# First scores by halves of the key/query ring, and row maxima turned by VectorE, in a fused transformer layer on one core

## The chip, the core and the metric

The kernel runs on one core of a Trainium2 chip. The metric is the device time of one execution in microseconds (us). TensorE (PE) does matmuls, VectorE (DVE) elementwise work and reductions, ScalarE (ACT) activations and copies, GpSimd (POOL) elementwise work, and SyncE (SP) only starts DMAs. ACT and POOL can start DMAs too. Every engine runs its own instructions in order, and semaphores tie the engines together. PSUM is the memory that TensorE writes: eight banks of 512 floats in each of 128 partitions.

## The reference, cut to what matters

```
x = x + attention(layernorm(x))     # 4 x 512 x 256, 16 heads of 16, biases, softmax over 512 keys
x = x + ffn(layernorm(x))           # silu(x W1') * (x W3'), Walsh-Hadamard transform over 1024, W2'
x = x + memory(layernorm(x))        # gate, scan with decay 0.95, query, output
x = x + ffn(layernorm(x))
scores  = einsum("bhqd,bhkd->bhqk", Q, K) / sqrt(16)
softmax = exp(scores - max over k) / sum over k
```

All of it is float32. The kernel splits each float32 operand into a high part (float32r) and a low part (the rest) and adds three products of parts, so that TensorE can run in its faster float32r form.

## The kernel before, in words

**Attention.** Batch `b` has 8 head pairs and 4 tiles of 128 tokens, so 32 steps (`STEPS`), and the loop variable `K` counts 128 steps over the four batches, with `s = K % 32`. A head of 16 channels stands as 48 rows in `ring`: three products of high and low parts of queries (`QI`) and keys (`KI`). Two heads share the 128 partitions: rows 0 to 47 (`blk` 0) and 64 to 111 (`blk` 1). `HALF` is 64. Rows `MROW` = 48 and 49 of each half hold minus the row maxima of the scores (high and low part) on the query side and ones on the key side, so that a second matmul over 50 rows gives score minus maximum.

**Two passes.** `score_qk(U, h)` computes queries by keys for step `U` and half `h`, into one of three banks (3 to 5), and DVE takes its negated maximum (`row_max`, tile `mxr`). `score_kq(K, h)` computes keys by queries with the maximum folded in, ACT takes the exponential (L735), and `weigh_values` multiplies by the values (`Vp`). The first pass runs 13 steps ahead (`LEAD`), so 26 scores are done before step 0. Eight steps make a group `S`, whose 16 columns of maxima must have become rows of `ring` before step `8 S`.

**How maxima become rows.** POOL splits the group's maxima into `ms` (L1071 and L1073, `split_max`), at steps with `s % 8 == 3`. TensorE transposes `ms` (L440, L472) into bank 7 (`MB`), which projections and others share, at `s % 8 == MAX_AT`. ACT copies it to `mT` (`max_evacuate`). SP starts two DMAs of `mT` into the rows (`max_rows`). Step `8 (S+1)` waits for `mrow_in`.

**Start.** DMAs bring in x, weights and constants. TensorE runs seven matmuls of ones (`keep_busy`) and then transposes the normalised first batch `XNs` (L396) as its four tiles come from DVE (`first_xns`). The projections follow: query and key tiles `n` = 0 to 3, of which 0 and 1 are the first heads' queries and keys, and then the values. ACT and DVE make the high and low parts `qh` and `ql` (for `n` = 2 and 3 in `AOh` and `AOl`), and DMAs spread them over `ring`: SP for `n` = 0, ACT for `n` = 1 (L704), six DMAs each. The first score waits for all twelve. `fly` is a butterfly on POOL for W2's Walsh-Hadamard transform (L1119, L1120), finished by four matmuls with `had` (`HAD_AT`) and two ACT copies each.

**Beside attention.** Projections of the next batch and of the output run inside the loop in `shared_bank`. POOL adds `ql`, `xTl`, `W2l` (L1051), the normalisation of the next batch (L1054; in batch 0 at `s` = 24 to 27, `NORM_AT`), `divide` (L1090) and the values' bias (L1080). Each is placed by step, and each engine takes them in the order of its loop body. TensorE transposes the next batch's `XNs` at `s` = 30 (`LN_AT[0]`, L292) and waits there for `xns_ready`.

After step 127 come the two FFNs and the memory layer; no line of theirs is touched.

Of the kernel before, what the change touches and what calls it, by code (L numbers as in the profile page):

```python
# [11 lines left out]
P = 128  # L12
# [5 lines left out]
GROUPS = 4  # L18
# [15 lines left out]
MAX_AT = 5  # L34
# [13 lines left out]
HAD_AT = (4, 5, 6, 8)  # L48
# [6 lines left out]
def build(nc, x, wq, wk, wv, wo, bqk_d, bv, bo, mv_, mg, mq, bgq_d, mo, w1, w2, w3, ident_d, had_d, out):  # L55
    ctx = ExitStack()
    with ctx:
# [36 lines left out]
        ms = sb("ms", [P, 2, 2, 2 * TT])  # L94
        mT = sb("mT", [32, P])
# [8 lines left out]
        spare = sb("spare", [P, 1])  # L104

# [19 lines left out]
        def quarter(slot, i):  # L125
# [5 lines left out]
        first_xns, wq_in, wk_in = (sem(n) for n in ("first_xns", "wq_in", "wk_in"))  # L131
# [12 lines left out]
        s1_ready, max_done, mh_done, ml_done, mps_ready, mt_ready, mrow_in = (  # L144
            sem(n) for n in ("s1_ready", "max_done", "mh_done", "ml_done", "mps_ready", "mt_ready", "mrow_in"))
# [11 lines left out]
        out_done = sem("out_done")  # L157
# [31 lines left out]
        def _(sp):  # L189
# [49 lines left out]
            max_rows(0)  # L239
            for b in range(BATCH):  # L240
# [38 lines left out]
        def _(pe):  # L279
# [55 lines left out]
            def score_qk(U, h):  # L335

                b, p, t = U // STEPS, U % STEPS // TT, U % TT
                i, blk = 2 * U + h, 1 - h
# [11 lines left out]
            def wait_qk(U, h):  # L350
                if U % 16 == 0 and h == 0:
                    b, mt = U // STEPS, U % STEPS // 16
                    pe.wait_ge(ring_in[2 * mt], QDMAS * (b + 1))
                    pe.wait_ge(ring_in[2 * mt + 1], QDMAS * (b + 1))
# [3 lines left out]
            def wait_kq(K, h):  # L358
                if K % 8 == 0 and h == 0:
                    pe.wait_ge(mrow_in, 2 * DMA * (K // 8 + 1))  # L360
                if K == 0 and h == 0:
                    pe.wait_ge(ones_in, 4 * DMA)
                j = 2 * K + h
# [7 lines left out]
            def weigh_values(a):  # L371
                S, kt = a // 4, a % 4
                g = S % GROUPS
                pe.wait_ge(exp_done, 4 * a + 4)
                if kt == 0:
# [15 lines left out]
            keep_busy(7, MB, SEQ)  # L391
# [9 lines left out]
            keep_busy(1, MB, SEQ)  # L401
# [16 lines left out]
            for U in range(LEAD):  # L418
                for h in range(2):
                    wait_qk(U, h)  # L420
                    score_qk(U, h)
                if U == 4:

                    pe.wait_ge(fly_done, 3)
                    pe.wait_ge(v_copied, 2)
                if U in HAD_AT:
                    j = HAD_AT.index(U)
                    mm(PS[:, HAD_BANK[j], :], had[:, :], PR[:, 4 + j, :], True, True).then_inc(had_ready, 1)
                elif U < 8:
                    keep_busy(1, MB, FILL)  # L430
                elif U == LEAD - 2:
                    pe.wait_ge(xns_ready, 1)
                    pe.wait_ge(mt_ready, 1)
                    ln_transpose(0, MB)
                else:
                    pe.wait_ge(w2h_done, 3)
                    keep_busy(1, PS[:, 2, :], FILL)
                if U == 8:
                    pe.wait_ge(ml_done, 1)
                    nc.tensor.transpose(MB[0:32, 0:P], ms[:, :, :, :].rearrange("p a b k -> p (a b k)"), ident[:, :])\  # L440
                        .then_inc(mps_ready, 1)
            pe.wait_ge(w2h_done, FT // 2)

            def shared_bank(K, b, s):

                more, turned = b < BATCH - 1, K + LEAD
                if s == LN_AT[0] and more:

                    pe.wait_ge(xns_ready, b + 2)
                    pe.wait_ge(mt_ready, turned // 8)  # L450
# [4 lines left out]
                if s % 8 == MAX_AT:  # L455
                    S = turned // 8 - 1
                    if S < LAST_GROUP:
                        pe.wait_ge(ml_done, S + 1)
                        pe.wait_ge(mt_ready, S)
                        if s // 8 == 0 and more:  # L460
                            pe.wait_ge(qk_f, 4 * b + 1)
                        elif s // 8 == 0:
                            pe.wait_ge(x_f, 2 * (b + 1))
                        elif s // 8 == 1 and more:
                            pe.wait_ge(qk_f, 4 * b + 3)
                        elif s // 8 == 2 and more:
                            pe.wait_ge(v_copied, 2 * (b + 1) + 1)
                        elif s // 8 == 2:
                            pe.wait_ge(x_done, 2 * b - 1)
                        elif more:  # L470
                            pe.wait_ge(v_copied, 2 * (b + 2))
                        nc.tensor.transpose(MB[0:32, 0:P], ms[:, :, :, :].rearrange("p a b k -> p (a b k)"),  # L472
                                            ident[:, :]).then_inc(mps_ready, 1)
                for n in range(4):
                    if s in QK_AT[n] and more:
                        if s == QK_AT[n][0]:
                            if n == 0:
                                pe.wait_ge(x_f, 2 * (b + 1))
                            elif n == 2:
                                pe.wait_ge(qk_f, 4 * b + 2)  # L480
                            else:
                                pe.wait_ge(mt_ready, turned // 8)
                        i = 3 * QK_AT[n].index(s)
                        project_qk(b + 1, n, range(i, i + 3))
                if s == OUT_AT[0][0] and b:
# [3 lines left out]
                    else:  # L489
                        pe.wait_ge(mt_ready, turned // 8)  # L490
                    for part in range(2):
                        out_projection(0, part)
                if s in OUT_AT[1] and b:
                    if s == OUT_AT[1][0]:
                        pe.wait_ge(mt_ready, turned // 8)
# [8 lines left out]
                if s in V_AT[1] and more:  # L504
                    if s == V_AT[1][0] and b:
                        pe.wait_ge(x_done, 2 * b)
                    elif s == V_AT[1][0]:
                        pe.wait_ge(mt_ready, turned // 8)
# [133 lines left out]
        def _(act):  # L642
# [17 lines left out]
            def qk_split(b, n):  # L660
                act.wait_ge(qk_f, 4 * (b - 1) + n + 1)
                act.wait_ge(ring_in[(n + 2) % 4], QDMAS * (b + (n > 1)))
# [7 lines left out]

            def max_evacuate(S):
                act.wait_ge(mps_ready, S + 1)
                if S:
                    act.wait_ge(mrow_in, 2 * DMA * S)
                hi(mT[:, :], MB[0:32, 0:P]).then_inc(mt_ready, 1)
# [20 lines left out]
            for n in range(4):  # L696
# [3 lines left out]
                if n == 1:  # L700
                    for part, ready in ((0, qk_hi), (1, qk_lo)):
                        act.wait_ge(ready, 2)
                        for args in ring_rows(0, 1, part):
                            act.dma_start(*args).then_inc(ring_in[1], DMA)  # L704
            for half in range(2):
                v_evacuate(0, half, PS[:, V_BANK[half], :])
            for n in range(2):
                act.wait_ge(ring_in[n], QDMAS)
# [519 lines left out]
```

## Time and profile before

| | us |
|---|---|
| median of 3 runs | 586.35 (586.34 to 586.47) |
| the profiled execution's own time | 586.26 |
| its span, first to last instruction | 584.4 |
| TensorE busy | 565.8 (97% of the span) |
| VectorE, ScalarE, GpSimd busy | 376.8, 298.5, 176.6 |
| granted TensorE clock over the span | 0.999 |

Busy time of an engine is the union of its instructions. TensorE's records overlap, so its busy share does not tell how much it streams; where one piece of its work ends and the next begins is read from starts. The time outside the span is 586.26 - 584.4 = 1.86 us.

### The profile page before, as it was taken

The page shows a single profiled execution, that of the slowest core. Times are in us where ns is not written, and L with a number is a line of the kernel's source. Part 1 is how long each engine was busy: PE and PEld are TensorE (multiplying, and loading weights), DVE is VectorE, ACT ScalarE, POOL GpSimd, SP SyncE. Part 2 cuts the span into 40 slices and gives each one's busy share as a digit, 9 for nine tenths or more (in the row PEclk, how much of TensorE's full clock was granted, in tenths as well). Part 3 has the DMA queues.
Part 4 walks back from the last instruction along what each step waited for, and adds up shares of the span by engine and source line. Part 5 has one row for each costly group of instructions (what it writes and reads, how often), then busy time and mean ns, then how long its engine had stood idle before and what let it go on. Part 6 is the DMA issues. An engine that isn't in the chain of part 4 may idle for free.

```text
span 584.4 us, 8867 instructions
## 1 busy us (share of the span) xinstructions
PE 565.8 (97%) x3288; PEld 390.1 (67%) x3288; DVE 376.8 (64%) x718; ACT 298.5 (51%) x546; POOL 176.6 (30%) x193
## 2 busy tenths in 40 slices
PE   9899999999999988999999999999999999999997
PEld 4534334344334433368888888898777888888886
DVE  5498898898888899644363444558887436344433
ACT  3238878876886787752334242244445233424221
POOL 3956446354455242820101010014333010101000
PEclk9999999999999999999999999999999999999999
DMA  7654740240033030010000000000000010010101
GB/s 231 135 112 163 199 122 18 76 127 20 2 111 109 3 146 3 3 72 2 1 0 1 1 0 1 2 2 0 1 0 2 1 36 1 1 36 2 38 0 37
DMA packets 17891, 26.54 MB, mean 45 GB/s; under 512 B 2552, under 2 KB 10744, under 8 KB 17464
## 3 DMA queue, kind: packets, MB, share of 16 engines
q1 hardware_dynamic: 15992, 24.13, 13.6%
q10 hardware_dynamic: 1856, 1.84, 1.4%
q8 instruction: 27, 0.44, 0.3%
q14 instruction: 16, 0.13, 0.1%
HBM read 10.88 MB, written 5.24 MB: 28 GB/s over the span
## 4 chain that ended last, share of the span: by engine, by line
PE 85%; DVE 5%; ACT 4%; issue 2%; DMA 1%; POOL 1%; SPq 1%; DVEq 0%; ACTq 0%
PE PS L281 82%; PE PS L292 2%; DVE mxr L861 2%; ACT PR L735 1%; DMA ring<-ql 1%; DVE PR L1020 1%; ACT xf L644 1%; ACT qf L658 1%; DVE XNs L842 1%; ACT PR L788 1%; POOL xTl L1051 1%; ACT xTh L644 1%; PE PS L472 1%; DVE AOl L853 1%; SPq L214 1%
## 5 line engine op out<-in xcount | busy, mean ns | idle before, releaser
L281 PE MATMUL PS<-xTh,ring 128*128 128x512 f32 x608 | 188.5, 392 | 0.0
L861 DVE TENSOR_REDUCE mxr<-PS 128x1 f32<-128x512 f32 x256 | 163.0, 682 | 29.0 <-PE PS L281 28.7
L735 ACT ACTIVATE PR<-PS 128x512 f32<-128x512 f32 x256 | 137.8, 603 | 39.7 <-PE PS L281 39.7
L281 PEld LDWEIGHTS PS<-xTh,ring 128*128 128x128 f32 x608 | 113.2, 188 | 22.9 <-issue 0.8
L281 PE MATMUL PS<-xTl,ring 128*128 128x512 f32 x304 | 110.3, 391 | 0.4 <-POOL xTl L1051 0.4
L281 PE MATMUL PS<-ring 50*128 50x512 f32 (+1 forms) x512 | 98.2, 450 | 5.4 <-DVE mxr L861 4.9
L975 DVE TENSOR_TENSOR PR<-PR,PS 128x512 f32<-128x512 f32 x64 | 43.8, 684 | 91.6 <-PE PS L281 73.7
L281 PEld LDWEIGHTS PS<-ring 50*128 50x128 f32 (+1 forms) x512 | 41.2, 184 | 84.2 <-ACT PR L735 57.2
L644 ACT ACTIVATE AOh<-PR 128x512 fp32r<-128x512 f32 x72 | 45.5, 632 | 101.1 <-DVE PR L975 89.2
L1051 POOL TENSOR_TENSOR xTl<-xf,xTh 128x512 fp32r<-128x512 f32 x30 | 43.2, 1456 | 140.9 <-ACT xTh L644 140.9
L853 DVE TENSOR_TENSOR AOl<-PR,AOh 128x512 fp32r<-128x512 f32 x72 | 51.1, 710 | 50.3 <-ACT AOh L644 50.3
L773 ACT ACTIVATE PR<-PS 128x512 f32<-128x512 f32 x64 | 38.0, 594 | 82.7 <-PE PS L281 82.6
L281 PE MATMUL PS<-W2h,AOh 128*128 128x256 f32 x256 | 72.4, 283 | 0.0
L281 PE MATMUL PS<-W2l,AOh 128*128 128x256 f32 x256 | 72.4, 283 | 0.0
L281 PE MATMUL PS<-W2h,AOl 128*128 128x256 f32 x256 | 72.2, 282 | 0.0
L281 PE MATMUL PS<-PR,Vp 128*32 128x512 f32 x512 | 68.2, 604 | 1.8 <-ACT PR L735 1.6
L281 PEld LDWEIGHTS PS<-xTl,ring 128*128 128x128 f32 x304 | 57.0, 188 | 11.0 <-POOL xTl L1051 0.8
L281 PEld LDWEIGHTS PS<-W2h,AOl 128*128 128x128 f32 x256 | 48.9, 191 | 1.9
L281 PEld LDWEIGHTS PS<-W2l,AOh 128*128 128x128 f32 x256 | 48.9, 191 | 1.9
L281 PEld LDWEIGHTS PS<-W2h,AOh 128*128 128x128 f32 x256 | 48.9, 191 | 0.0
L1044 POOL TENSOR_TENSOR veps<-mom,eps 128x4 f32<-128x4 f32 x16 | 3.2, 200 | 128.4 <-DVE mom L832 128.3
L1090 POOL TENSOR_TENSOR OTn<-OT,rec 128x256 f32<-128x256 f32 x16 | 9.9, 620 | 64.2 <-DVE rec L908 64.2
(98 smaller groups left out, 621.5 us busy)
## 6 DMA issues: line engine op xcount, KB each, us to landing
ring<-qh SPq DMA_DIRECT2D x52, 128.0 KB, 3.1
ring<-ql SPq DMA_DIRECT2D x26, 128.0 KB, 3.1
ring<-weight_scratch SPq DMA_DIRECT2D x3, 1024.0 KB, 4.9
weight_scratch<-in_w SPq DMA_DIRECT2D x2, 1024.0 KB, 6.8
out<-X SPq DMA_DIRECT2D x8, 256.0 KB, 2.2
X<-in_x SPq DMA_DIRECT2D x3, 512.0 KB, 5.2
PR<-in_w SPq DMA_DIRECT2D x1, 1024.0 KB, 7.6
ring<-AOh SPq DMA_DIRECT2D x8, 128.0 KB, 4.0
```

The source lines that it names most:

```text
L214: sp.dma_start(*args).then_inc(ring_in[n], DMA)
L281: return nc.tensor.matmul(dst, lhsT, rhs, start=start, stop=stop, skip_group_check=True)
L292: last = nc.tensor.transpose(bank[:, t * P:(t + 1) * P], XNs[:, t, dt * P:(dt + 1) * P], ident[:, :])
L472: nc.tensor.transpose(MB[0:32, 0:P], ms[:, :, :, :].rearrange("p a b k -> p (a b k)"), ident[:, :]).then_inc(mps_ready, 1)
L644: return nc.scalar.activation(dst, src, ACT.Copy, scale=scale)
L735: nc.scalar.activation(PR[:, j % 8, :], PS[:, kq_bank(j), :], ACT.Exp, scale=HD ** -0.5)\
L773: nc.scalar.activation(PR[:, f % 2, :], PS[:, f % 2, :], ACT.Silu).then_inc(sg_done, 1)
L853: return nc.vector.tensor_tensor(dst, src, h.bitcast(F32), ALU.subtract)
L861: nc.vector.tensor_reduce(mxr[:, S % 2, blk, TT * p + t:TT * p + t + 1], PS[:, QK0 + i % 3, :], AX.X, ALU.max, negate=True).then_inc(max_d ...
L975: nc.vector.tensor_tensor(PR[:, 2 + f % 2, :], PR[:, f % 2, :], PS[:, 2 + f % 2, :], ALU.mult)\
L1051: return nc.gpsimd.tensor_tensor(dst, src, h.bitcast(F32), ALU.subtract)
L1090: nc.gpsimd.tensor_tensor(OTn[:, :, c:c + HD], OT[:, :, 0:HD], rec[:, :].unsqueeze(2).broadcast_to([P, SEQ // 32, HD]), ALU.mult)\
```

## The change

**Scores.** `score_qk` takes every fourth query (`t:SEQ:TT`) as its stationary operand instead of 128 neighbours. The first 16 scores come in the order: all eight steps of half `h` = 0 (`blk` 1), and then all eight of `h` = 1 (`first_score`). **Ring rows.** SP starts all twelve first DMAs, those of `blk` 1 ahead of those of `blk` 0, with a semaphore for each half (`first_rows`); ACT starts none. The eight DMAs of `wo` move from ACT to SP, behind the first group's maxima. **Maxima.** `ms` becomes 128 x 4 x 32 and is zeroed once; DVE transposes it in blocks of 32 x 32 into `mT` (`turn_max`); TensorE's transposes and ACT's copies of maxima go. The rows are moved by eight DMAs of one row and four partitions each: four from SP and four from POOL (`max_rows` on POOL, directly behind `split_max`). **Start.** `keep_busy` is 4 instead of 7 matmuls at first, and 1 instead of 5 ahead of the scores; the matmuls with `had` move to steps 8, 9, 10 and 12; the normalisation of batch 1 moves from POOL to ACT (two passes of four activations); the parts of `WO` are made in steps 3 and 5.

```diff
-MAX_AT = 5
+MAX_AT = 4
-HAD_AT = (4, 5, 6, 8)
+HAD_AT = (8, 9, 10, 12)
-        ms = sb("ms", [P, 2, 2, 2 * TT])
-        mT = sb("mT", [32, P])
+        ms = sb("ms", [P, TT, 32])
+        mT = sb("mT", [P, P])
+        def first_score(i):
+
+            return (i % 8, i // 8) if i < 16 else (i // 2, i % 2)
+
+        def max_row_copies(S, blk):
+
+            b, g = S // GROUPS, S % GROUPS
+            return [(ring[HALF * blk + MROW + k:HALF * blk + MROW + k + 1, b % 2, QI, 2 * g + p, :].bitcast(F32),
+                     mT[16 * p + 2 * blk + k:P:32, :]) for k in range(2) for p in range(2)]
...
             def max_rows(S):
-
-                b, g = S // GROUPS, S % GROUPS
                 sp.wait_ge(mt_ready, S + 1)
-                for blk in range(2):
-                    r = HALF * blk + MROW
-                    sp.dma_start(ring[r:r + 2, b % 2, QI, 2 * g:2 * g + 2, :].bitcast(F32),
-                                 mT[16 * blk:16 * blk + 16, :]).then_inc(mrow_in, DMA)
+                for to, src in max_row_copies(S, 0):
+                    sp.dma_start(to, src).then_inc(mrow_in, DMA)
...
-            ring_load(0, 0)
-
-            for n in range(2):
-                sp.wait_ge(ring_in[n], QDMAS)
+
+            for blk in (1, 0):
+                for n in range(2):
+                    copies = ring_rows(0, n, 0)[2 * blk:2 * blk + 2]
+                    sp.wait_ge(qk_hi, n + 1)
+                    for args in copies:
+                        sp.dma_start(*args).then_inc(first_rows[blk], DMA)
+                    copies = ring_rows(0, n, 1)[blk:blk + 1]
+                    sp.wait_ge(qk_lo, n + 1)
+                    for args in copies:
+                        sp.dma_start(*args).then_inc(first_rows[blk], DMA)
             ring_load(0, 2)
             ring_load(0, 3)
             max_rows(0)
+
+            for e in range(2):
+                for j in range(GH):
+                    r = 32 * j + HD * e
+                    sp.dma_start(OT[r:r + HD, :, :].rearrange("p a c -> p (a c)").rearrange("p (g n) -> p g n", n=D),
...
-                mm(PS[:, QK0 + i % 3, :], ring[r:r + KROWS, b % 2, QI, p, t * P:(t + 1) * P],
+
+                mm(PS[:, QK0 + i % 3, :], ring[r:r + KROWS, b % 2, QI, p, t:SEQ:TT],
...
-            keep_busy(7, MB, SEQ)
+            keep_busy(4, MB, SEQ)
...
-            keep_busy(1, MB, SEQ)
+            keep_busy(1, MB, FILL)
...
-            keep_busy(2, PS[:, 5, :], SEQ)
-            pe.wait_ge(ring_in[0], QDMAS)
-            keep_busy(3, PS[:, 5, :], SEQ)
+            keep_busy(1, PS[:, 5, :], SEQ)
             pe.wait_ge(qk_hi, 4)
             pe.wait_ge(qk_lo, 4)
...
-                if s % 8 == MAX_AT:
-                    S = turned // 8 - 1
-                    if S < LAST_GROUP:
-                        pe.wait_ge(ml_done, S + 1)
-                        pe.wait_ge(mt_ready, S)
...
-                        nc.tensor.transpose(MB[0:32, 0:P], ms[:, :, :, :].rearrange("p a b k -> p (a b k)"),
-                                            ident[:, :]).then_inc(mps_ready, 1)
...
+            act.wait_ge(nmean_done, 1)
+            act.wait_ge(rstd_done, 2)
+            act.wait_ge(lnT_ready, 2)
+            for t in range(TT):
+                nc.scalar.activation(XNs[:, t, :], X[:, TT + t, :], ACT.Identity, bias=nmean[:, t:t + 1])\
+                    .then_inc(centred, 1)
...
             for j in range(FT // 2):
                 if j == FT // 2 - 1:
-                    max_evacuate(0)
+                    ln_evacuate(1, 0, MB)
+                    ln_hi(1, 0, 0)
...
+            def turn_max(S):
+
+                dve.wait_ge(ml_done, S + 1)
+                if S:
+                    dve.wait_ge(mrow_in, 4 * DMA * S)
+                    dve.wait_ge(mrow_in2, 4 * DMA * S)
+                nc.vector.transpose(mT[:, :].rearrange("p (i t) -> p t i", t=TT), ms[:, :, :]).then_inc(mt_ready, 1)
...
+                if s % 8 == 3 and (K + 5) // 8 < LAST_GROUP:
+                    turn_max((K + 5) // 8)
...
+            def max_rows(S):
+
+                pool.wait_ge(mt_ready, S + 1)
+                for to, src in max_row_copies(S, 1):
+                    pool.dma_start(to, src).then_inc(mrow_in2, DMA)
...
                 if s % 8 == 3 and (K + 5) // 8 < LAST_GROUP:
                     split_max((K + 5) // 8)
+                    max_rows((K + 5) // 8)
```

TensorE's program at the first scores. `AOf` is the tile of ones of `keep_busy`, `ring` the scores. Before:

```order
L281 MATMUL PS<-AOf 128x512 x2
L281 MATMUL PS<-AOf 128x512 [waits ring_in0]
L281 MATMUL PS<-AOf 128x512 x2
L281 MATMUL PS<-ring 128x512 [waits ring_in0,ring_in1,qk_lo,qk_hi]
L281 MATMUL PS<-ring 128x512
L281 MATMUL PS<-AOf 128x384
```

The changed kernel at the same place:

```order
L305 MATMUL PS<-AOf 128x512
L305 MATMUL PS<-ring 128x512 [waits first_rows1,qk_lo,qk_hi]
L305 MATMUL PS<-ring 128x512
L305 MATMUL PS<-AOf 128x384
L305 MATMUL PS<-ring 128x512
L305 MATMUL PS<-ring 128x512 [waits max_done]
```

Four matmuls of ones have gone, and the first score waits for one half's rows instead of two tiles' rows.

POOL's program at the end of batch 0 (`s` = 26 to 28): the third tile of the normalisation, the split of the maxima, the low part of the attention output, the last tile of the normalisation (which signals `xns_ready`) and the values. Before:

```order
L1054 TENSOR_SCALAR XNs<-X,mom,rstd 128x256
L1071 CAST ms<-mxr 128x2x8 [waits mps_ready,max_done]
L1073 TENSOR_TENSOR ms<-mxr,ms 128x2x8 [waits mh_done]
L1051 TENSOR_TENSOR AOl<-AOf,AOh 128x512 [waits aoh_done]
L1054 TENSOR_SCALAR XNs<-X,mom,rstd 128x256
L1080 TENSOR_TENSOR Vp<-vst,bvt 128x4x4x16 [waits av_done,v_copied] x2
```

The changed kernel:

```order
L1061 TENSOR_SCALAR XNs<-X,mom,rstd 128x256
L1082 CAST ms<-mxr 128x2x2x4 [waits mt_ready,max_done]
L1084 TENSOR_TENSOR ms<-mxr,ms 128x2x2x4 [waits mh_done]
L1090 DMA ring<-mT 1x4x128 [waits mt_ready]
L1090 DMA ring<-mT 1x4x128 x3
L1058 TENSOR_TENSOR AOl<-AOf,AOh 128x512 [waits aoh_done]
L1061 TENSOR_SCALAR XNs<-X,mom,rstd 128x256
L1097 TENSOR_TENSOR Vp<-vst,bvt 128x4x4x16 [waits av_done,v_copied] x2
```

Four DMAs, behind a wait for DVE's transpose, now stand ahead of the last tile of the normalisation.

DVE's program at steps 9 to 12 of the changed kernel (before, the same rows without `mT<-ms`):

```order
L909 STREAM_TRANSPOSE OT<-PS 128x512 [waits wol_done,av_done]
L857 TENSOR_REDUCE mxr<-PS 128x1 [waits s1_ready] x2
L913 RECIPROCAL rec<-OT 128x16 [waits ot_done]
L857 TENSOR_REDUCE mxr<-PS 128x1 [waits ml_done,s1_ready]
L857 TENSOR_REDUCE mxr<-PS 128x1 [waits s1_ready]
L866 STREAM_TRANSPOSE mT<-ms 128x4x32 [waits mrow_in2,mrow_in,ml_done]
L857 TENSOR_REDUCE mxr<-PS 128x1 [waits s1_ready] x12
```

The new transpose waits for POOL's split (`ml_done`), and twelve maxima are queued behind it.

## Rows read from the trace of the kernel before

**Rows 1.** By stretch: length, busy PE, PEld, DVE, ACT, POOL; clock, DMA share, GB/s.

```profile
96.74:151.26 54.52, 53.83 (x345) 23.42 (x341) 47.41 (x86) 42.95 (x85) 25.28 (x31) 1.00 0.19 60
251.00:584.40 333.40, 327.35 (x1896) 286.32 (x1896) 172.87 (x350) 120.91 (x200) 48.20 (x46) 1.00 0.03 10
```

**Rows 2.** Chain that ended last, to 45 us: start us, us, what.

```profile
1.44 8.74 PE PS L281 x14
...
18.20 6.24 DMA ring<-ql
```

**Rows 3.** Timeline, 6 to 21 us: start us, us, engine, line.

```profile
6.89 1.38 DVE L842 TENSOR_SCALAR XNs<-X,mom,rstd 128x256 f32<-128x256 f32 x4 [1.48 <-POOL rstd L1047]
8.72 0.63 ACT L644 ACTIVATE WAh<-xf 128x512 fp32r<-128x512 f32 x1 [0.65 <-DMA xf<-in_wv]
11.65 1.09 ACT L644 ACTIVATE xTh<-PS 128x512 fp32r<-128x512 f32 x2 [2.30 <-PE PS L396]
14.94 2.57 SPq L214 DMA_DIRECT2D ring<-qh  x4
```

**Rows 4.** Timeline of PE, 12 to 46 us.

```profile
12.70 0.40 PE L281 MATMUL PS<-xTh,WAh 128*128 128x512 f32 x1
12.94 0.39 PE L281 MATMUL PS<-xTh,WAl 128*128 128x512 f32 x1
...
20.95 1.88 PE L281 MATMUL PS<-AOf 128*128 128x512 f32 x4
24.48 2.84 PE L281 MATMUL PS<-AOf 128*128 128x512 f32 x6 [1.65 <-DMA ring<-ql]
27.25 0.50 PE L281 MATMUL PS<-ring 48*128 48x512 f32 x2
...
28.53 0.51 PE L281 MATMUL PS<-ring 48*128 48x512 f32 x2
...
33.84 0.50 PE L281 MATMUL PS<-ring 48*128 48x512 f32 x2
...
35.33 0.51 PE L281 MATMUL PS<-ring 48*128 48x512 f32 x2
...
44.78 0.74 PE L281 MATMUL PS<-ring 50*128 50x512 f32 x4
```

**Rows 5.** Timeline of PE, steps 5 and 7 (51 to 57 us), and its weight loads.

```profile
51.98 0.74 PE L281 MATMUL PS<-ring 50*128 50x512 f32 x4
...
53.12 1.07 PE L281 MATMUL PS<-PR,Vp 128*32 128x512 f32 x8
...
55.67 0.74 PE L281 MATMUL PS<-ring 50*128 50x512 f32 x4
55.67 0.30 PEld L281 LDWEIGHTS PS<-ring 50*128 50x128 f32 x4 [0.36 <-ACT PR L735]
56.34 1.07 PE L281 MATMUL PS<-PR,Vp 128*32 128x512 f32 x8
```

**Rows 6.** Timeline of DVE and POOL, step 11.

```profile
62.70 1.29 DVE L861 TENSOR_REDUCE mxr<-PS 128x1 f32<-128x512 f32 x2
...
64.91 0.22 POOL L1073 TENSOR_TENSOR ms<-mxr,ms 128x16 fp32r<-128x16 f32 x1
```

**Rows 7.** Timeline of POOL and PE, steps 27 to 30.

```profile
91.28 0.22 POOL L1073 TENSOR_TENSOR ms<-mxr,ms 128x16 fp32r<-128x16 f32 x1
...
92.72 1.22 POOL L1054 TENSOR_SCALAR XNs<-X,mom,rstd 128x256 f32<-128x256 f32 x1
...
94.49 0.66 PE L292 MATMUL PS<-ident,XNs 128*128 128x128 f32 x4
```

**Rows 8.** Tile `mT`, and POOL by form: count, min/median/max ns; busy us, mean ns.

```profile
L222 SPq DMA_DIRECT2D ring<-mT x32: 610/654/686, 40.1 to 239.2; - x32
...
L1047 POOL TENSOR_TENSOR rstd<-veps,mhalf 128x4 f32<-128x4 f32 x16 | 16.2, 1014 | 1.3
```

**Rows 9.** Chain that ended last, step 119.

```profile
239.20 1.92 DMA ring<-mT
```

More of the change, by code:

```diff
@@ L143, in build @@
         ring_in = [sem(f"ring_in{n}") for n in range(4)]
[L144 to L145 removed]
+        first_rows = [sem(f"first_rows{blk}") for blk in range(2)]
+        s1_ready, max_done, mh_done, ml_done, mt_ready, mrow_in = (
+            sem(n) for n in ("s1_ready", "max_done", "mh_done", "ml_done", "mt_ready", "mrow_in"))
         st_ready, exp_done, av_done, ot_done, rec_done, otn_done, aof_ready, aoh_done, aol_done, wo_ready, x_done = (
@@ L442, in _ @@
-            pe.wait_ge(w2h_done, FT // 2)
+            for i in range(2 * LEAD):
+                U, h = first_score(i)
+                if i in (0, 8):
+                    pe.wait_ge(first_rows[1 - h], QDMAS)
+                if i >= 3:
+                    pe.wait_ge(max_done, i - 2)
+                score_qk(U, h, i)
+                if i % 2 and U < 8:
+                    keep_busy(1, MB, FILL)
+                elif i % 2:
+                    if U == 8:
+                        pe.wait_ge(fly_done, 3)
+                        pe.wait_ge(v_copied, 2)
+                    if U in HAD_AT:
+                        j = HAD_AT.index(U)
+                        mm(PS[:, HAD_BANK[j], :], had[:, :], PR[:, 4 + j, :], True, True).then_inc(had_ready, 1)
+                    if U == LEAD - 2:
+                        pe.wait_ge(xns_ready, 1)
+                        ln_transpose(0, MB)
@@ L493, in shared_bank @@
                 if s in OUT_AT[1] and b:
-                    if s == OUT_AT[1][0]:
-                        pe.wait_ge(mt_ready, turned // 8)
+                    if s == OUT_AT[1][0] and more:
+                        pe.wait_ge(v_copied, 2 * (b + 1) + 1)
+                    elif s == OUT_AT[1][0]:
+                        pe.wait_ge(x_done, 2 * b - 1)
                     out_projection(1, OUT_AT[1].index(s))
@@ L699, in _ @@
                     .then_inc(qk_hi, 1)
[L700 to L704, printed above, removed]
             for half in range(2):
                 v_evacuate(0, half, PS[:, V_BANK[half], :])
-            for n in range(2):
-                act.wait_ge(ring_in[n], QDMAS)
-            for e in range(2):
-                for j in range(GH):
-                    r = 32 * j + HD * e
-                    act.dma_start(OT[r:r + HD, :, :].rearrange("p a c -> p (a c)").rearrange("p (g n) -> p g n", n=D),
-                                  wo.rearrange("(g e) (j c) n -> e j c g n", e=2, c=32)[e, j, 0:HD, :, :])\
-                        .then_inc(wo_in, DMA)
+            act.wait_ge(nmean_done, 1)
[4 more added lines that the diff above has]
+                    .then_inc(centred, 1)
+            for t in range(TT):
+                c = slice(TT + t, TT + t + 1)
+                act.wait_ge(centred, t + 1)
+                last = nc.scalar.activation(XNs[:, t, :], XNs[:, t, :], ACT.Copy, scale=rstd[:, c])
+            last.then_inc(xns_ready, 1)
             for j in range(FT // 2):
                 if j == FT // 2 - 1:
-                    max_evacuate(0)
+                    ln_evacuate(1, 0, MB)
+                    ln_hi(1, 0, 0)
                 act.wait_ge(had_ready, j + 1)
@@ L893, in _ @@
                     .then_inc(qk_lo, 1)
-            for U in range(LEAD):
-                for h in range(2):
-                    row_max(U, h)
+            for i in range(2 * LEAD):
+                row_max(*first_score(i), i)
+                if i == 16:
+                    turn_max(0)
             def transpose_out(S):
```

120 lines of the change are left out of this document (45 added, 75 removed).

## The prediction

> **What bounds the kernel now.** I read the windows by stretch first, since a share over the whole span hides stages with different limits. From 251 us on, TensorE is busy 327 of 333 us and every other engine about half of that or less [rows 1]; no line of that stage is touched, so I cost it at nothing. Inside a batch TensorE is again nearly always busy, but VectorE is busy 47.4 of 54.5 us and ScalarE 43.0 [rows 1]: TensorE bounds, with VectorE's maxima close behind. Next the chain that ended last, for the start: TensorE's fills to 10 us, projections, then a DMA of `ring` that lands 6.24 us after its issue [rows 2]. The timeline shows what this costs: the values end at 20.95, fills and an idle gap of 1.65 us follow, the first score starts at 27.25 and step 0 at 44.78 [rows 4]. Last come the steps with `s % 8` of 3 and 5, one with the split, one with TensorE's transpose [rows 5, 6], and the end of batch 0, where POOL's last normalised tile comes just ahead of the matmuls that need it [rows 7].
>
> **The change, part by part: before the first score.** Fourteen records of fills (two for each of seven matmuls) run to 1.44 + 8.74 = 10.18 us, slower before the clock is granted in full [rows 2]. Eight records would end near 7.4. Not all of that comes back: `XNs` is ready at 6.89 + 1.38 = 8.27, and ACT is held by weights from a DMA until 8.72 + 0.63 = 9.35 before it can copy `xTh`, which it started at 11.65 [rows 3]. So `xTh` moves 2.3 us earlier, with a shorter fill 2.4, and all projections with it. SP's issues of rows started at 14.94, four of them in 2.57, so 0.64 each [rows 3]. They now start at 12.5, and the six of `blk` 1 (the other tile's among them) are issued by about 16.3. The values end at 20.95 - 2.4 = 18.55; a fill takes about 0.5 more, and low parts are ready by then. The DMA of rows that took 6.24 us ran with all twelve, at full DMA load. Six ought to land within some 3 us, by 19.3. I take the first score at 19.5, 7.7 us earlier. The other half's six are issued by 20.1, land by about 23.2, and are wanted eight scores later, at 25.5: hidden, with 2 us of cover.
>
> **From the first score to step 0.** Before, a round of two scores and a fill took 28.53 - 27.25 = 1.28 us, one with `had` 35.33 - 33.84 = 1.49 [rows 4]. The two scores of a round stood in different halves of the rows and ran side by side: 0.50 us for both. In the new order the first eight rounds take both from one half, one after the other; consecutive matmuls of 512 columns start 0.24 apart (12.70, 12.94) [rows 4]. So I add 0.23 to 1.28: eight rounds of 1.50, 12.0 us. Then come three rounds with `had` (4.5), one with neither (1.0), one more with `had` (1.5): 19.0 us, against 44.78 - 27.25 = 17.53. Step 0 starts at 19.5 + 19.0 = 38.5, 6.3 us earlier. ACT's last copies of `W2h` now stand later, behind `xTh` of batch 1, and cost the first exponentials an estimated 0.6. **Start: -5.7.** POOL's part (butterfly, then split, then rows) ends some 5 us ahead of step 0, at any price of its DMAs up to 1.3 us.
>
> **Inside the batches: what goes.** A step with TensorE's transpose of maxima takes 53.12 - 51.98 = 1.14 us to its values' matmuls, one without 56.34 - 55.67 = 0.67 [rows 5]: 0.47 back. Two of four per batch are like that; in the other two a projection stands beside it and my reading there is 0.38. That is 1.70 per batch. In batch 0 the last disappears in a stall (below), 1.32; in batch 3 TensorE waits more often for VectorE and I count 0.44. ACT's copies lie in its idle time.
>
> **What comes, on VectorE.** `turn_max` moves 128 x 128 floats, an estimated 0.35 us with its wait. It waits for POOL's split, and behind it are queued the maxima that TensorE's scores wait for (a ring of three banks). At step 11 the previous maxima end at 62.70 + 1.29 = 63.99 and the split at 64.91 + 0.22 = 65.13 [rows 6]: VectorE stands 1.14 us, then turns for 0.35. The banks cover about 1.1 of it; I put 0.4 on TensorE. It happens at step 11 of batches 0 to 2 and step 19 of batch 0: 1.6. At the other steps POOL is ready first.
>
> **What comes, on POOL.** Four DMAs per group. No row shows a DMA from POOL. The nearest are SP's, of the same tiles, at a median 0.654 us of queue time each; a tiny POOL instruction of 128 x 4 takes 1.014 [rows 8]. I take c = 0.8 each, between them; below 0.61 there is no reason to go, upwards there is no firm bound. Their main victim is the end of batch 0. The split ends at 91.28 + 0.22 = 91.50, then come `AOl` (to 92.72) and the last `XNs` (1.22, to 93.94), and TensorE's four transposes at 94.49 [rows 7]. Now the turn (0.35) and 4c stand in between: 91.50 + 0.35 + 4c + 1.22 + 1.22, with semaphores 94.35 + 4c, is 97.55 at c = 0.8. TensorE waits **3.06 us** (2.5 at 0.65, 3.9 at 1). In later batches the normalisation stands at `s` = 19 and is done before.
>
> The rows themselves must land before the next step with `s % 8` = 0. A DMA of `mT` lands 1.92 us from the start of its issue [rows 9], so about 1.3 after its end: the split's end + 0.35 + 4c + 1.3. Step 32 starts at 96.74 [rows 1], 5.24 after the split's end; the need is 4.85 at c = 0.8. It just fits, and I count 0.3 in all, in batch 3.
>
> **Sum.** Batch 0: -1.32 + 0.8 + 3.06 = +2.5. Batches 1 and 2: -1.70 + 0.4 = -1.3 each. Batch 3: -0.44 + 0.3 = -0.1. Together -0.2. In the tail, step 120's rows came at 239.20 + 1.92 = 241.12 [rows 9]; any gain there is met by POOL's later low part, and I count nothing. With the start, -5.9 against the profiled 586.26, which is 0.09 below the median of the runs: **580.4 us**.
>
> **A rule against the change.** `score_qk` now reads every fourth query as its stationary operand. The trace has no strided load; contiguous ones show four loads in 0.30 us of a step whose scores take 0.67 [rows 5], and I price the strided ones the same. The Trainium skill ("Advanced Engine Details and Errata", section "Memory Cachelines") says that SBUF needs two hits on a 16-byte line to run at full speed; four floats are 16 bytes, so each element here would be on its own line. By that rule the penalty exists and rival 2 below is the result; by the row alone it is zero.
>
> **Rivals.**
> 1. *POOL's DMAs are dear.* At c = 1 the batch-0 wait grows by 0.8, rows come late at most groups (together some 1.9) and the tail adds 0.6: 583.7. At c = 1.1 each of some 11 groups is late by about 0.4 more than that: 588.7; at 1.3, 599. It turns slower from c of about 1.05. For it: a POOL instruction with next to no data takes 1.01 [rows 8]. Against: issuing a DMA moves no data through the engine. The Trainium skill ("DMA: Bandwidth & Descriptors", section "Latency and other measured facts") puts a DMA of GpSimd's path at about 1 us to its first byte against 0.6; read as c, this gives 583.7.
> 2. *The strided load costs.* Loads of a pair of scores are exposed by some 0.11 us each. If a load takes twice as long, about 230 pairs lose 0.107 each, 24.6 us: 605; a quarter of that penalty already brings 586.5. For it: no cover beside scores. Against: a load reads one column of 128 at a time, and four loads took only 0.30 [rows 5]. It decides from a quarter of the doubling.
> 3. *The clock falls* to its lower level because fewer fills run before the scores. It would cost about 5 us, 585. Against: the gap of 1.65 us [rows 4] left the granted clock at full.
> 4. *The first rows land no faster than before*, 6.24 us after issue. The first score is then at 22 and the time 582.8: the halving does half of its work.
> 5. *The batch-0 wait is smaller*, because POOL's DMAs cost 0.6 or TensorE reaches the transposes later anyway: 577 to 578.5.
>
> **How the numbers follow.** The forecast, with rival 5 inside it, has 0.58 and a range of its own of 577.5 to 583.5. Rival 1 has 0.14, most of it above 586; rival 2 0.16; rival 3 0.05; rival 4 0.07. A measurement of this kernel can tell about 0.2% (1.2 us) from no change. Faster, below 585.2: the forecast, rival 4, part of 3 and of 1, 0.72. Same, to 587.5: 0.06. Slower: most of rivals 1 and 2, 0.22. The range for 8 in 10 goes from 575.5, where the first score comes sooner or the batch-0 wait is half, to 590, where rival 1 stands at c = 1.1 or rival 2 at two fifths of its penalty.
>
> **What the profile of the changed kernel would show.** The first score at 19.5 (22 or later: rival 4) and step 0 at 38.5; rounds of 1.50 with pairs of scores no longer side by side. POOL's DMAs of `ring<-mT` at 0.8 apart. VectorE's transpose standing about 1.1 us at step 11. At `s` = 30 of batch 0 some 3 us of idle time before TensorE's four transposes, ended by `XNs`, and none at that place in batches 1 and 2. No idle time that `mT` ended at `s` = 0 mod 8. Steps of 0.67 us with `s` = 5, where 1.14 stood. Weight loads of scores as long as before (0.30 for four; 0.45 or more: rival 2). Granted clock at 1.00 from 7 us on (else rival 3). The forecast is wrong if any of the three unshown prices is off: POOL's DMA beyond 1.0 us, the strided load, or the landing of the first six rows.

## The result, and the profile after

The changed kernel is slower: 612.87 us in the median of 4 runs (608.62 to 615.07) against 586.35 (4 runs), ratio 1.0447 with a 95% interval of 1.0384 to 1.0511. The forecast was 580.4 with a range of 575.5 to 590. The profiled execution took 611.29 us with a span of 609.7, 25.3 above the 584.4 of before, at a mean granted clock of 0.972.

The windows of the changed kernel, cut where the granted clock moves. Columns: stretch, length, then busy time and count of PE, PEld, DVE, ACT and POOL, granted clock, DMA share, GB/s.

```profile
0.00:23.30 23.30, 18.62 (x76) 12.25 (x76) 11.81 (x34) 8.35 (x13) 13.75 (x19) 1.00 0.83 206
23.30:47.20 23.90, 23.90 (x38) 8.64 (x36) 11.79 (x19) 3.16 (x8) 5.54 (x5) 0.50 0.46 75
...
57.40:60.90 3.50, 3.50 (x15) 1.07 (x14) 2.10 (x4) 2.70 (x6) 1.66 (x3) 0.51 0.69 249
...
112.00:118.90 6.90, 6.90 (x32) 2.48 (x24) 3.81 (x7) 4.25 (x8) 3.15 (x3) 0.51 0.01 2
118.90:609.00 490.10, 478.05 (x2806) 357.45 (x2802) 306.65 (x585) 239.04 (x422) 144.16 (x175) 1.00 0.08 25
```

Three stretches of 34 us together ran at the lower level, 0.50 of full speed (1.2 of 2.4 GHz). Before, the clock was at 1.00 in every stretch of [rows 1]. Busy shares do not show this: TensorE is busy all the time in the slow stretches, since its matmuls last longer (two fills of 384 columns take 1.65 us there, and 0.91 at the full clock in run e3 below). The first and the third stretch begin within 2 us of the end of a wait of TensorE, of 2.84 and 2.18 us. The second, from 57.4 us, does not: the longest idle time of TensorE in the 10 us ahead of it is 0.36 us. No run explains that one.

TensorE's timeline, first scores, one round at each clock, and the first score of steps 0, 32, 64 and 96 (the answers to [rows 4] and [rows 7]).

```profile
22.73 0.93 PE L305 MATMUL PS<-ring 48*128 48x512 f32 x2 [2.84 <-DMA ring<-ql]
23.59 1.65 PE L305 MATMUL PS<-AOf 128*128 128x384 f32 x2
25.17 1.24 PE L305 MATMUL PS<-ring 48*128 48x512 f32 x2
...
47.14 0.63 PE L305 MATMUL PS<-ring 48*128 48x512 f32 x2
...
48.76 0.63 PE L305 MATMUL PS<-ring 48*128 48x512 f32 x2
...
53.37 0.62 PE L305 MATMUL PS<-ring 50*128 50x512 f32 x2
...
110.18 0.66 PE L316 MATMUL PS<-ident,XNs 128*128 128x128 f32 x4 [2.18 <-POOL XNs L1061]
...
112.99 0.82 PE L305 MATMUL PS<-ring 50*128 50x512 f32 x2
...
172.06 0.62 PE L305 MATMUL PS<-ring 50*128 50x512 f32 x2
...
228.80 0.62 PE L305 MATMUL PS<-ring 50*128 50x512 f32 x2
```

Set beside the starts of before, the 25.3 us arise like this: 8.6 up to step 0 (53.37 against 44.78), 7.7 in batch 0, 4.6 in batch 1, 2.2 in batch 2, 2.3 from step 96 to the end. The first score is 4.5 us earlier than before (22.73 against 27.25), but 30.6 us lie from it to step 0, where 17.5 lay. That the loss goes on in every batch, also where the clock is full, says that there are at least two causes.

The first rows came late. From the chain, the DMA whose issue starts at 16.97 lands 5.62 us later:

```profile
16.97 5.62 DMA ring<-ql
22.59 0.14 issue
```

Last, the two prices that no row of before showed. Weight loads of the first pass by form, and the tile `mT` (count, minimum, median and maximum ns of one):

```profile
L305 PEld LDWEIGHTS PS<-ring 48*128 48x128 f32 x256 | 58.5, 308 | 15.5 <-DVE mxr L857 9.5 <-issue 6.0
...
L1090 POOL DMA_DIRECT2D ring<-mT x64: 566/566/810, 46.6 to 262.9; - x64
L866 DVE STREAM_TRANSPOSE mT<-ms x16: 397/405/456, 45.9 to 260.3; 128x128 f32<-128x128 f32 x16
```

A strided load takes 308 ns on average. A DMA from POOL takes 0.57 us (four in 2.3 to 2.5), less than SP's 0.654 in [rows 8]: my first rival, dear DMAs, is out.

### The profile page after: what moved, and what is told of

The parts are those of the page before. It is cut to its first block, busy times and chain, and to the rows that moved or that the text cites. A ratio compares the mean times of both kernels' runs of the same rounds, so it can differ in the third digit from the quotient of the medians.

```text
span 609.7 us, 8908 instructions
## 1 busy us (share of the span) xinstructions
PE 588.6 (97%) x3258; PEld 409.5 (67%) x3258; DVE 384.2 (63%) x734; ACT 302.3 (50%) x538; POOL 208.8 (34%) x255
## 4 chain that ended last, share of the span: by engine, by line
PE 75%; POOL 8%; issue 6%; DVE 5%; ACT 4%; DMA 2%; SPq 0%; POOLq 0%; DVEq 0%
PE PS L305 72%; PE PS L316 2%; POOL ring L1090 2%; ACT PR L729 1%; DMA ident<-in_ident_d 1%; DMA ring<-ql 1%; DVE ring L932 1%; POOL xTl L1058 1%; POOL W2l L1058 1%; POOL ql L1058 1%; POOL XNs L1061 1%; ACT xf L649 1%; POOL X L1118 1%; DVE mxr L857 1%; DVE PR L1027 1%
## 5 line engine op out<-in xcount | busy, mean ns | idle before, releaser
L305 PE MATMUL PS<-ring 48*128 48x512 f32 (+1 forms) x512 | 121.6, 499 | 7.8 <-DVE mxr L857 4.6
L305 PEld LDWEIGHTS PS<-ring 48*128 48x128 f32 (+1 forms) x512 | 62.4, 251 | 93.2 <-ACT PR L729 57.2
L305 PE MATMUL PS<-PR,Vp 128*32 128x512 f32 x512 | 70.1, 620 | 3.0 <-DVE OT L909 1.8
L1090 POOL DMA_DIRECT2D ring<-mT x64 | 37.2, 583 | 14.7 <-DVE mT L866 14.7
```

The costliest lines, as they stand in the source:

```text
L305: return nc.tensor.matmul(dst, lhsT, rhs, start=start, stop=stop, skip_group_check=True)
L1090: pool.dma_start(to, src).then_inc(mrow_in2, DMA)
```

## The experiments

Theory A, formed from this trace: the strided load costs about 0.1 us in each step, and a gap ahead of the first score loses the clock. Theory B is the clock alone, theory C the load alone, theory D that the new thin rounds lose the clock whatever stands ahead of them. Where the stationary operand is changed without the rows' layout, the maxima land at other queries' places: a softmax does not depend on what is subtracted, only its safety against overflow does, and these kernels are for timing.

### e1 and e2: the load apart

```diff
-  mm(PS[:, QK0 + i % 3, :], ring[r:r + KROWS, b % 2, QI, p, t:SEQ:TT],
+  mm(PS[:, QK0 + i % 3, :], ring[r:r + KROWS, b % 2, QI, p, t * P:(t + 1) * P],
```

e1 applies this to the changed kernel, e2 its inverse to the kernel before. Of e1:

> The changed kernel with the scores' stationary operand read as before, 128 neighbouring queries (the maxima then stand at other queries' places, so that the output is another; the number and kind of instructions is the same). Theory A, two causes, strided loads and a lost clock: the load falls from 307 to about 187 ns, a pair of scores with its maximum-folded pair from 0.46 to 0.34 us, 0.12 for each of 128 steps, 15 us: about 598 us, and the clock still falls behind the wait for the first rows. Theory B, the clock alone: above 608 us. Theory C, the strided load alone (the clock falls because of it): below 590 us and a clock at 1.00.

Of e2:

> The kernel before with every fourth query as stationary operand and nothing else changed (maxima at other queries' places, so another output). Theory A: 128 steps longer by 0.12 us each, 586.35 + 15.4 = about 602 us, with the clock at 1.00 throughout. Theory B (the load is hidden): 586 to 588 us. Theory C: the clock falls in this kernel too, over 605 us.

e1 took 604.21 us (ratio to before 1.0326, 1.0291 to 1.036), 8.7 below the changed kernel where theory A said 15, and still with a clock of 0.969: in its trace the first stretch at the lower clock is 27 us long, against 23.9. e2 took 599.0 (1.0227, 1.0209 to 1.0244), with the clock at 0.999. Loads of the first pass by form, in the kernel before and in e2:

```profile
L281 PEld LDWEIGHTS PS<-ring 48*128 48x128 f32 x256 | 37.7, 184 | 7.5 <-DVE mxr L861 5.9 <-issue 1.5
```

```profile
L281 PEld LDWEIGHTS PS<-ring 48*128 48x128 f32 x256 | 54.8, 307 | 7.5 <-DVE mxr L861 6.0 <-issue 1.5
```

The one edit adds 123 ns to each load and 599.0 - 586.2 = 12.8 us to the kernel, 0.1 us for each of 128 steps. B and C are out: the load costs by itself, and without it the clock still falls.

### e3, f1 and f4: the gap and the clock

```diff
-            keep_busy(1, PS[:, 5, :], SEQ)
+            keep_busy(15, PS[:, 5, :], SEQ)
```

> The changed kernel with 15 fills instead of 1 behind the values, so that TensorE has work through the 2.84 us in which it waited for the first rows. Theory A (the gap lets the clock fall): the first score at about 22.8 us as now, the rounds at 1.6 instead of 2.75 us, step 0 at about 43 instead of 53.4: 612.9 - 10 = about 602 us, with the later two falls still there. Theory D (the thin rounds of scores, 48 rows of one half one after another, lose the clock whatever stands ahead): 611 to 614 us, the clock falls within the rounds.

It took 610.39 us (1.0408, 1.0378 to 1.0438), nearly as much as the changed kernel, so the number alone would have spoken for D. The timeline says otherwise:

```profile
19.50 13.04 PE L305 MATMUL PS<-AOf 128*128 128x512 f32 x30
32.47 0.85 PE L305 MATMUL PS<-ring 48*128 48x512 f32 x2
33.25 0.91 PE L305 MATMUL PS<-AOf 128*128 128x384 f32 x2
34.09 0.85 PE L305 MATMUL PS<-ring 48*128 48x512 f32 x2
...
53.29 0.86 PE L305 MATMUL PS<-ring 50*128 50x512 f32 x4
```

The rounds are down from 2.75 to 1.62 us and the clock is full until 111 us. I had taken a fill for 0.22 us where it is 0.87, so the fills ran 9.7 us past the rows' landing and spent what the clock gave. f1 is the same edit with 5:

> The changed kernel with 5 fills behind the values instead of 1. In the run with 15 a fill (two records) took 0.87 us, not 0.22 as I had reckoned, so that 15 of them ran to 32.5 us, 9.7 us past the rows' landing, and ate what the held clock gave. Theory A: five cover the gap of 2.84 us, first score at 23.6, rounds at 1.62 us, step 0 at about 44.4 instead of 53.4: 612.9 - 9 = about 604 us. Theory D (thin rounds lose the clock by themselves): the clock falls within the rounds, above 609 us.

f1 took 600.33 us (1.0265, 1.0223 to 1.0308), 12.5 below the changed kernel, with step 0 at 44.97 instead of 53.37. So the trace shows 8.4 us of the 12.5 at the start. Of the rest it shows nothing, since the profiled execution of f1 was its slowest (605.2, clock 0.988; the others 0.993 to 0.997): by these clocks, what is lost later differs from one execution to the next. This one also lost the clock for 7 us behind a wait at step 16:

```profile
74.12 1.24 PE L305 MATMUL PS<-ring 50*128 50x512 f32 x4 [1.59 <-DMA ring<-mT]
```

The reverse, taking all five fills ahead of the first score out of the kernel before:

```diff
-            keep_busy(2, PS[:, 5, :], SEQ)
             pe.wait_ge(ring_in[0], QDMAS)
-            keep_busy(3, PS[:, 5, :], SEQ)
```

> The kernel before without the five fills ahead of the first score, so that TensorE stands from 20.95 us until the rows land at 24.5, 3.5 us instead of 1.65. Theory A (a gap of some 3 us loses the clock, in this kernel too): first score at 24.6 instead of 27.25, but the clock falls within the rounds and they take about 2.2 us instead of 1.28 and 1.49: step 0 at 50 to 52, 591 to 594 us. Theory D (only the new, thinner rounds lose it): the clock stays, 584 us.

It took 588.5 us (1.0047, 1.0019 to 1.0076; single executions 584.96 to 591.21). Timeline of TensorE, and windows:

```profile
25.83 0.80 PE L281 MATMUL PS<-ring 48*128 48x512 f32 x2 [4.70 <-DMA ring<-ql]
26.55 1.65 PE L281 MATMUL PS<-AOf 128*128 128x384 f32 x2
```

```profile
23.60:30.40 6.80, 4.57 (x8) 1.60 (x8) 2.58 (x4) 0.00 (x0) 6.80 (x6) 0.50 0.68 120
30.40:45.40 15.00, 15.00 (x48) 5.75 (x47) 13.54 (x22) 6.22 (x12) 6.67 (x9) 1.00 0.57 115
```

A gap of 4.7 us loses the clock in the kernel before too, so a gap can do it without the new rounds, and in e3 and f1 the new rounds pass at the full clock: D is out as the cause of the first fall. Two things came out otherwise than expected. The first score could start only at 25.83 and not at 24.6, and the fall was short: step 0 starts at 45.40, not at 50 to 52. Here the clock is back after 6.8 us, and within two rounds of the old kind; in the changed kernel it stayed down for 23.9 us, up to the rounds with `had`. That the thin rounds keep it down is what these traces suggest, and g3 below, with the old order and a fall of 10 us, fits it; no run isolates it. The five fills were no waste: in the median they are worth 2.6 us (588.5 against 585.92 for the kernel before, run beside it).

### e6, f0, f2: both edits, and a third cause

> The changed kernel with both edits: neighbouring queries as stationary operand (another output) and the wait filled. Theory A: 612.9 - 15 - 10 = about 587 us, what is left above the forecast being the wait for normalised tiles at the end of batch 0, its loss of clock, and first rows that land later than I said. If a third cause is hidden, above 592 us.

e6 took 602.33 us (1.0278, 1.0246 to 1.031), 15 more than expected. The same miscounted fills are 9.1 of it (f0 below, with 5 fills, takes 593.22). Most of the rest stands in the chain and timeline of step 16:

```profile
68.04 0.52 SPq L273
...
74.71 4.71 DMA ring<-mT
```

```profile
79.47 0.75 PE L305 MATMUL PS<-ring 50*128 50x512 f32 x4 [2.38 <-DMA ring<-mT]
```

The rows of group 2 are 16 KB in all. SP's four DMAs stand in its queue behind 1 MB of X and 768 KB of ring rows, and the last takes 4.71 us to land, where one took 1.92 in [rows 9]. POOL's four have a queue of their own and are no faster (68 to 80 us, size of one and median us to landing):

```profile
ring<-mT POOLq DMA_DIRECT2D x4, 2.0 KB, 4.4
```

So it is not the place in SP's queue alone: the bulk transfers fill the DMA engines (a share of 1.11 from 72 to 74.4 us). TensorE waits 2.4 us, and the clock falls behind that wait (80.96 to 91.2 us at 0.5). f0 is this kernel with 5 fills, and f2 also moves the two loads of X behind the rows:

```diff
-                    if b == 0 and s == 9:
+                    if b == 0 and s == 13:
                         sp.wait_ge(w2l_done, FT // 2)
                         for c in range(2, BATCH):
                             sp.dma_start(X[:, c * TT:(c + 1) * TT, :], xv[c, :, :, :])...
```

> The changed kernel with neighbouring queries as stationary operand, 5 fills, and SP's two loads of X (1 MB) moved from step 9 to step 13, behind the rows of maxima. In the run with the first two edits and 15 fills TensorE stood 2.4 us at step 16 for rows whose DMA took 4.7 us to land beside those loads, and the clock then fell for 10 us. Theory A: no wait at step 16, clock at 1.00 until the end of batch 0; step 0 at 42, batch 0 at 54.5 us instead of 60.9, the rest as in that run: about 585 us. Rival: the rows are late from the eight small DMAs themselves, the wait at step 16 stays at 2 us or more and the time is above 589.

> f2 without the move of the loads of X. Theory A (the rows of group 2 queue behind 1 MB of X): a wait of 1.5 to 2.4 us for rows at step 16 and a fall of the clock behind it, 591 to 594 us against 589.1. Rival (the move did nothing): 589 us and no wait at step 16.

f0 took 593.22 us (1.0127, 1.0109 to 1.0146), with a wait of 2.19 us at step 16; f2 589.09 (1.0054, 1.0034 to 1.0075; 587 where the clock held; 585 was expected), with none. The move is worth 4 us. From 63 to 65 us the DMA share was 1.12 and 1.07 in f0 (one value for each us), and 0.44 and 0.64 in f2, where POOL's row DMAs landed in 2.1 us. In f2 the first score starts at 23.47 and step 0 at 42.64: 19.2 us, where the forecast's sum said 19.0. What f2 still waits for is the end of batch 0, here with the clock at 1.00 before and after:

```profile
96.17 0.66 PE L316 MATMUL PS<-ident,XNs 128*128 128x128 f32 x4 [2.41 <-POOL XNs L1061]
```

### f3 and g1: POOL's queue at the end of batch 0

f3 puts POOL's last normalised tile ahead of the split and its DMAs at step 27.

```diff
-                if s % 8 == 3 and (K + 5) // 8 < LAST_GROUP:
+                if s % 8 == 3 and (K + 5) // 8 < LAST_GROUP and K != 27:
...
+                if K == 27:
+                    split_max(4)
+                    max_rows(4)
```

> The kernel of the run above, and in batch 0 POOL takes the fourth tile of the normalisation ahead of the split and its four DMAs (step 27). Theory A: the wait of 2.2 to 2.8 us ahead of TensorE's transposes at step 30 goes, and with it the fall of the clock that follows it; the rows of that group land by about the start of step 32: 2 to 5 us below the run above, 580 to 583 us. Rival: the rows come late at step 32 by as much, and nothing is gained.

It took 592.42 us (1.011, 1.0092 to 1.0128), 3 us more than f2. The wait moved, and not to the rows: VectorE's queue, then TensorE's.

```profile
92.81 0.40 DVE L866 STREAM_TRANSPOSE mT<-ms 128x128 f32<-128x128 f32 x1 [3.64 <-POOL ms L1084]
```

```profile
93.84 0.51 PE L305 MATMUL PS<-ring 50*128 50x512 f32 x2 [2.82 <-DVE mxr L857]
```

`turn_max` stands 3.64 us for the split, the maxima are queued behind it, and TensorE runs out of banks. g1 leaves the split where it was and has SP start all eight DMAs of groups 4 and 15, the two whose DMAs on POOL delay something else (the counts that the waits on `mrow_in` and `mrow_in2` compare with are changed to match):

```diff
-                for to, src in max_row_copies(S, 0):
+                for to, src in max_row_copies(S, 0) + (max_row_copies(S, 1) if S in (4, 15) else []):
                     sp.dma_start(to, src).then_inc(mrow_in, DMA)
...
-                    max_rows((K + 5) // 8)
+                    if (K + 5) // 8 not in (4, 15):
+                        max_rows((K + 5) // 8)
```

> The kernel of f2 (neighbouring queries, 5 fills, X later; median 589.1, 587.0 in the executions with the clock at 1.00) with the four row DMAs of groups 4 and 15 started by SP behind its own four, not by POOL. POOL then gives the last normalised tile 2.3 us sooner at the end of batch 0, and starts the low parts of the tail 2.4 us sooner. Theory A (these two places are what is left of the cost of POOL's DMAs): the wait of 2.4 us at step 30 falls under 0.5, and the 1.7 us at step 123 go; SP's eight DMAs take 4.4 us, so that rows land at about the start of step 32: 589.1 - 4 = about 585 us, and with fewer falls of the clock down to 583. Rival: the rows come late at step 32 by 1 to 2 us, 587 to 588.

It took 584.43 us (0.9981, 0.9967 to 0.9995; 584.1 to 585.1 in nine of ten executions, with the clock at 1.00). The wait at step 30 is gone; what is left is 0.44 us at step 32:

```profile
96.47 0.74 PE L310 MATMUL PS<-ring 50*128 50x512 f32 x4 [0.44 <-DMA ring<-mT]
```

The tail shows the second place. In the changed kernel POOL's low parts of the weights start only after its DMAs, at 263.52 us, and lie beside VectorE's casts, five of which take 7.61 us (before: five in 5.69); the transpose of `OT` queued behind them comes late:

```profile
261.53 7.61 DVE L932 CAST ring<-ring 128x512 fp32r<-128x512 f32 x5
...
270.51 1.07 PE L305 MATMUL PS<-PR,Vp 128*32 128x512 f32 x8 [1.84 <-DVE OT L909]
```

The 7.61 us are not five slow casts: one record alone has 6.28 of them, while POOL ran four subtractions in a row (263.52 to 268.52), and before the longest cast took 1.50. In g1 TensorE waits 0.98 us for rows at step 120 and 0.27 at the later place, and from the first score of step 120 to the first matmul of the FFN it takes 10.83 us, against 10.84 before and 11.94 in the changed kernel.

### g3 and g2: the order, and another stride

g3 is f2 with the first 16 scores in the old order (`first_score` returns `(i // 2, i % 2)`, and both halves' rows are awaited at the first two).

> f2 with the first 16 scores in the old order, half by half within a step, so that the first score waits for both halves' rows. Theory: the second half's rows, issued to 21.4, land at 25 to 26 us; rounds take 1.28 us instead of 1.50; step 0 at 25.7 + 17.7 = 43.4 instead of 42.6, and the wait of 2 us or more ahead of it may lose the clock: 590 to 592 us. If the new order's thinner rounds cost as much as its earlier start gives: 589 us.

It took 594.79 us (1.0172, 1.0117 to 1.0228), 5.7 more than f2. One half's rows were there at 23.31, the other's kept TensorE waiting 4.20 us, to 27.98; the clock fell for 10 us, and step 0 came at 49.53. The new order does what it was said to do: in f2 the second half's scores start at 29.44, so the same landing is hidden. How much of the 5.7 is the order and how much the clock it lost is not told apart.

g2 changes in the kernel before only the stationary slice, to every second query:

```diff
-                mm(PS[:, QK0 + i % 3, :], ring[r:r + KROWS, b % 2, QI, p, t * P:(t + 1) * P],
+                mm(PS[:, QK0 + i % 3, :], ring[r:r + KROWS, b % 2, QI, p, 256 * (t // 2) + t % 2:256 * (t // 2) + 256:2],
```

> The kernel before with every second query as stationary operand (two of the four floats of 16 bytes are used). If two hits on a 16-byte line are enough for full speed, loads stay at 185 ns and the time at 586.3 us. If a load pays by the lines that it touches, half of the extra of a stride of four: loads at about 220 ns, 590 to 593 us. If any stride costs the same: 599 us.

It took 586.6 us (1.001, 0.9998 to 1.0022), with loads of 192 ns:

```profile
L281 PEld LDWEIGHTS PS<-ring 48*128 48x128 f32 x256 | 38.8, 192 | 7.4 <-DVE mxr L861 5.9 <-issue 1.5
```

A stride of two floats costs nothing that can be told from the noise (8 ns in a load, and an interval of the time that includes no change), a stride of four 12.8 us. That is the pattern that the Trainium skill gives ("Advanced Engine Details and Errata", section "Memory Cachelines"): two hits on a 16-byte line are enough, one is not.

## Why the prediction was wrong

The forecast was 32.5 us too low. Two terms of its sum stood at nothing and were not nothing, the strided load and the clock, and a third, the landing of the first rows, was sized too small.

**The strided load: the step that failed first.** "Contiguous ones show four loads in 0.30 us ..., and I price the strided ones the same." A load of the first pass takes 308 ns instead of 184; by e2 that alone costs 12.8 us. The mechanism stood in rival 2 with a chance of 0.16, and its price there was too high by a factor of about two, since I took about 230 pairs where there are 128 steps with one pair each (0.1 us apiece, 12.8 us in all). The rule of the Trainium skill ("Advanced Engine Details and Errata", section "Memory Cachelines") was quoted for it and these runs agree with it; the case against it ("a load reads one column of 128 at a time") came from no row.

**The first rows: "Six ought to land within some 3 us, by 19.3."** The six issues ended at 17.57, 1.3 us after the 16.3 of the forecast; the last row landed 5.62 us after its issue began. The six DMAs of the other half, issued behind them, ran beside them, and from 17 to 23 us the DMA share was 1.08. That they slowed the first six fits this, but no run left them out. This was rival 4. The first score came 4.5 us earlier where 7.7 was forecast, and 2.1 of the 4.5 are not the halving but the earlier projections (`xTh` starts at 9.57 instead of 11.65). The other half was forecast to land by 23.2; in g3 it landed at 27.98.

**The clock: "the gap of 1.65 us [rows 4] left the granted clock at full."** True of that gap, but the gap became 2.84 us as soon as rival 4 came true, and the fills that used to cover it were taken out by the change itself. I gave rivals 3 and 4 separate chances (0.05 and 0.07), where the one brings the other with it, and priced the fall at 5 us. Filling the gap gave 12.5 us in the median (f1), 8.4 of them by step 0. The cause of the first fall is shown from both sides: none where the gap was filled (e3, f1), and one in the kernel before when its gap was widened to 4.70 us (f4).

**What held, and what was off by little.** The sum from first score to step 0 (19.0 forecast, 19.2 in f2, with neighbours and a full clock). The wait at the end of batch 0: the formula 94.35 + 4c against 94.49 gives 2.1 us at the measured c of 0.57, and TensorE waited 2.18; I had 3.06 because I took 0.8. But I did not add that such a wait loses the clock again: it fell at 112 us for 6.9 us. `turn_max` stood 0.99 us at step 11 where 1.14 was forecast. The gain in each of batches 1 and 2 is 0.9 us (f2, 53.6 against 54.5) and not 1.3. Batch 3, forecast at -0.1, is longer: 36.56 us up to step 120 in f2, against 35.40. The tail, counted at nothing, cost 1.1 us.

**What was not seen.** The rows behind the 1 MB of X at step 16, worth 4 us once the start is early enough for them to meet; my range of landing times came from one undisturbed DMA, 1.92 us [rows 9].

So the 26.5 us are, by the runs: 8.4 to 12.5 for the lost clock at the start (f1), 9 to 13 for the load (e1, e2), and the rest for the waits on POOL and in the tail and for two later falls of the clock, less a true gain at the start (2.1 us in f2, 42.64 against 44.78) and in batches 1 and 2. The parts overlap: at the low clock a load is hidden differently, and e1's 8.7 us come with more clock lost than in the changed kernel. How they divide to the last microsecond stays open.

The change's parts other than the load are worth something only together with their cover: with neighbouring queries, 5 fills, X behind the rows and SP's DMAs in two groups the kernel takes 584.43 us, 0.19% less than before. It is no finished version, since its maxima belong to other queries. As `max_row_copies` moves the rows, in four pieces of 128 queries from blocks of 32 x 32, they come in order only at a stride of four, which is the stride that costs. Whether a stride of two with smaller pieces would pay was not tried.

## What to carry to other kernels

When a change takes out filler work and also moves a transfer, ask how long TensorE stands if the transfer lands late, and price the lost clock with it, not apart. A stationary operand with a new stride is an unmeasured price on every matmul that uses it: multiply it by the count before anything else, and measure it alone. A blocking wait moved onto a busy engine stalls what is queued behind it, and giving POOL's work a better order only moved that stall to VectorE and TensorE; giving the DMAs to an idle queue removed it.

## What was not expected of the hardware

- Weight loads of 48 partitions by 128 float32: 184 ns for neighbours, 192 at a stride of two, 307 at a stride of four.
- Waits of TensorE of 1.59 us (f1, step 16) to 4.70 us (f4) were followed by a granted clock of 0.5 in these traces, for 3.4 to 27 us. Waits of 1.65 us [rows 4], 1.84 (changed kernel, tail), 1.99 (e1, step 16) and 2.41 (f2) were not, and the fall at 57.4 us of the changed kernel has no wait ahead of it. The length of a gap alone does not decide it.
- Row DMAs of 2 KB, normally landed in 1.6 us, took up to 4.7 beside bulk transfers, those from POOL's own queue as well (median 4.4).
- A DMA issued by POOL takes 0.57 us of its queue, by SP 0.49 for the same rows.
- Of VectorE's eight casts of 128 x 512 in the changed kernel the median took 0.44 us, one took 1.50, and one 6.28 us, during which POOL ran four subtractions of the same size in a row.
